# Layer 1's loop: one pair of three multiplies XW in 32 bits in tiles with one gathered tile, and the split of XW becomes a ring

## What is computed

```python
XW = X @ W
s_col = XW @ a[0, :f];  s_row = XW @ a[0, f:]
Z1 = leaky_relu(s_row[:, None] + s_col[None, :], 0.01)
den = exp(Z1)
num = A @ den
att = where(num != 0, den / num, 0)
H = A @ (att @ XW)
x = layernorm(x + H)
```

## Time and profile before

| | |
|---|---|
| median of 3 runs | 705.02 us (704.59 to 706.17) |
| profiled execution | 705.56 us, span 703.8 us |
| PE | 591.9 us busy, 84% of the span |
| DVE | 573.3 us, 81% |
| ACT | 442.3 us, 63% |
| POOL | 407.3 us, 58% |
| layer 1's loop | about 414 to 624 us of the span |

### The profile page before, as it was taken

One profiled execution on the slowest core, in us unless ns is written; L12 is line 12 of the kernel. 1 busy time (PEld: TensorE's weight loads), 2 busy tenths in 40 slices (PEclk: granted clock), 3 DMA queues, 4 the chain that ended last, 5 costly groups with the idle time before them and its releaser, 6 DMA issues.

```text
span 703.8 us, 11521 instructions
## 1 busy us (share of the span) xinstructions
PE 591.9 (84%) x4211; PEld 351.9 (50%) x4211; DVE 573.3 (81%) x1044; ACT 442.3 (63%) x689; POOL 407.3 (58%) x449
## 2 busy tenths in 40 slices
PE   4499999999999697999745988798989988868993
PEld 4343333333333296888635644344434444436883
DVE  1689999999999875578878866899999999985442
ACT  2378888888888551478995416777776777721000
POOL 5448888877778704445602163877576777002663
PEclk9999999999999769999955999999999999987998
DMA  9974444484000000000000041233232323000100
GB/s 146 101 78 41 40 36 37 37 297 150 1 1 1 5 2 8 16 24 17 17 9 12 13 116 50 74 105 87 68 91 77 97 72 84 17 5 8 30 28 16
DMA packets 17796, 37.20 MB, mean 53 GB/s; under 512 B 2570, under 2 KB 8222, under 8 KB 17726
## 3 DMA queue, kind: packets, MB, share of 16 engines
q0 software_dynamic: 7392, 24.32, 20.0%
q1 hardware_dynamic: 10334, 11.98, 5.2%
HBM read 48.72 MB, written 10.45 MB: 84 GB/s over the span
## 4 chain that ended last, share of the span: by engine, by line
PE 37%; DVE 35%; issue 15%; ACT 8%; POOL 2%; DMA 2%; DVEq 0%; POOLq 0%; ACTq 0%; SPq 0%
DVE ring L849 8%; PE PSALL L1727 8%; DVE R L858 7%; PE PSALL L1625 7%; PE PSALL L1440 6%; DVE ring L1255 4%; PE PSALL L1686 3%; ACT AW L603 3%; DVE ring L1248 3%; PE PSALL L1421 2%; PE PSALL L1371 2%; PE PSALL L1633 2%; ACT R L700 2%; DVE FR L1255 1%; PE PSALL L1499 1%
## 5 line engine op out<-in xcount | busy, mean ns | idle before, releaser
L399 POOL TENSOR_TENSOR R<-R,ring 128x452 f32<-128x452 f32 (+1 forms) x126 | 151.6, 1205 | 33.2 <-ACT ring L531 31.6
L858 DVE SCALAR_TENSOR_TENSOR R<-ring,R 128x452 bf16<-128x452 f32 (+1 forms) x132 | 134.6, 1021 | 0.0
L1421 PE MATMUL PSALL<-R,AO 128*128 128x452 bf16 (+2 forms) x396 | 99.5, 360 | 16.1 <-DVE R L858 15.1
L531 ACT ACTIVATE ring<-ring,sm 128x452 f32<-128x452 f32 (+1 forms) x132 | 88.4, 670 | 27.8 <-DVE ring L849 21.0
L1371 PE MATMUL PSALL<-XN 128*128 128x452 f16 (+2 forms) x396 | 99.3, 362 | 4.7 <-issue 4.2
L459 POOL DMA_INDIRECT AW<-ATd,FR x44 | 62.7, 1426 | 64.3 <-PE PSALL L1633 39.9
L1625 PE MATMUL PSALL<-AW,R 128*128 128x452 fp8e4 (+1 forms) x348 | 78.5, 357 | 24.9 <-DVE R L1187 18.6
L539 ACT ACTIVATE R<-ring,sm 128x452 bf16<-128x452 f32 (+1 forms) x132 | 88.6, 671 | 4.3
L849 DVE TENSOR_TENSOR ring<-PSALL,AT 128x452 f32<-128x452 f32 (+1 forms) x132 | 81.0, 613 | 0.9 <-PE PSALL L1371 0.9
L1686 PE MATMUL PSALL<-ring,X 128*128 128x452 bf16 (+1 forms) x300 | 67.8, 360 | 0.9 <-DVE ring L1255 0.9
L1421 PEld LDWEIGHTS PSALL<-R,AO 128*128 128x128 bf16 (+1 forms) x396 | 28.5, 97 | 76.2 <-DVE R L858 61.9
(11 more groups left out here) (253 smaller groups left out, 1033.1 us busy)
## 6 DMA issues: line engine op xcount, KB each, us to landing
AT<-in_adjT POOLq DMA_DIRECT2D x22, 338.5 KB, 7.7
ATd<-AT SPq DMA_DIRECT2D x2, 3723.5 KB, 17.3
XWd<-ring SPq DMA_DIRECT2D x11, 128.0 KB, 1.8
out<-ring SPq DMA_DIRECT2D x21, 64.0 KB, 1.5
AW<-ATd,FR POOLq DMA_INDIRECT x44, 4.3
X<-XWd,idx POOLq DMA_INDIRECT x22, 3.2
Wt<-in_W SPq DMA_DIRECT2D x1, 64.0 KB, 11.1
X<-in_x SPq DMA_DIRECT2D x1, 0.5 KB, 7.9
```

The lines of the kernel that those rows point to most:

```text
L399: i = G.tensor_tensor(ES_, ES_, z, ALU.add)
L858: V.scalar_tensor_tensor(F[0:rows, RW:RW + w], z, 1.0, F[0:rows, 0:w], ALU.subtract, ALU.subtract).then_inc(s_low, 1)
L1421: m = TE.matmul(PSALL[:, c, 0:w], half_[0:rows, jt, :], F[0:rows, o:o + w], start=(jt == 0 and k == 0), stop=(jt == T - 1 and k == 2))
```

## The change

- PE: the middle pair of a tile (`p % 3 == 1`) is multiplied by XW in 32 bits where `kinds[jt] == 0`: one matmul per chunk (`xw_full`) in place of three. The other pairs and the two-tile tiles keep the three (`xw_halves`). Two branches on PE choose.
- DVE: for that pair of a one-tile tile no low half is computed; a branch skips it, and a memset of one element reports it as done. The second gathered block's scores and halves are computed only if the next tile has two blocks, under a branch; the halves are one operation of 128 columns each. For that DVE loads `win[jt]` into a register, once a tile.
- ACT: the Exp of the denominators covers two blocks, and the third under a branch, with its own register load. The wait for DVE's scores stands before the branch.
- GpSimd: XW itself stays as it is in 32 bits; its halves go to a ring of four tiles, `XW2`, with two operations in place of three. From tile 4 on they wait until the products of tile t - 4 are through (`s_y`).

```diff
+        XW2 = sb("XW2", [P, 4, 2, D], BF16)
+        mark = sm[0:1, 13:14]
             def split_xw(t):
-                gp.wait_ge(s_ohl[0], T)
-                gp.wait_ge(s_perm[0], 1)
                 gp.wait_ge(s_AT[t], 32)
-                if t:
-                    gp.wait_ge(s_xws, 3 * t)
-                G.tensor_copy(iota[:, :], XWs[:, t, :]).then_inc(s_xws, 1)
-                gp.wait_ge(s_xws, 3 * t + 1)
-                G.tensor_tensor(XWh[:, t, :, 0], XWs[:, t, :], iota[:, :], ALU.subtract).then_inc(s_xws, 1)
-                gp.wait_ge(s_xws, 3 * t + 2)
-                G.tensor_copy(XWh[:, t, :, 1], iota[:, :]).then_inc(s_xws, 1)
+                if t >= 4:
+                    gp.wait_ge(s_y, 3 * (t - 3))
+                G.tensor_copy(XW2[:, t % 4, 1, :], XWs[:, t, :]).then_inc(s_xws, 1)
+                gp.wait_ge(s_xws, 2 * t + 1)
+                G.tensor_tensor(XW2[:, t % 4, 0, :], XWs[:, t, :], XW2[:, t % 4, 1, :], ALU.subtract).then_inc(s_xws, 1)
             def den_exp_small(jt):
+                kind = eng.value_load(win[0:1, jt:jt + 1], min_val=0, max_val=2)
                 av.wait_ge(s_denz, 3 * (jt + 1))
                 s = T + jt % 2 * DS
-                S.activation(den_w[:, s:s + DS, :], den_w[:, s:s + DS, :], ACT.Exp).then_inc(s_dene, 1)
+                met = av.covered()
+                with eng.If(kind == 1):
+                    S.activation(den_w[:, s + 2, :], den_w[:, s + 2, :], ACT.Exp)
+                av.only(met)
+                S.activation(den_w[:, s:s + 2, :], den_w[:, s:s + 2, :], ACT.Exp).then_inc(s_dene, 1)
+            def score(jt, q):
+                s = T + jt % 2 * DS
+                return V.tensor_scalar(den_w[:, s + 1 + q, :], cb3[:, jt, :], Rw[:, q, jt:jt + 1], r01w[:, q, jt:jt + 1],
+                                       ALU.add, ALU.max)
+            def half_of(jt, q):
+                s = T + jt % 2 * DS
+                return V.tensor_tensor(den_h[:, s + 1 + q, :, 0], den_w[:, s + 1 + q, :], den_h[:, s + 1 + q, :, 1], ALU.subtract)
-            def small_scores(jt):
+            def small_scores(jt, usual):
                 s = T + jt % 2 * DS
                 if jt >= 2:
                     dv.wait_ge(s_num, 6 * (jt - 1))
                 dv.wait_ge(s_pick, 2 if jt < FIRST else 4)
+                if usual:
+                    kinds[jt] = eng.value_load(win[0:1, jt:jt + 1], min_val=0, max_val=2)
+                    met = dv.covered()
+                    with eng.If(kinds[jt] == 1):
+                        score(jt, 1)
+                    dv.only(met)
+                    score(jt, 0).then_inc(s_denz, 2)
...
-            def small_halves(jt):
+            def small_halves(jt, usual):
                 s = T + jt % 2 * DS
                 dv.wait_ge(s_dene, jt + 1)
+                if usual:
+                    met = dv.covered()
+                    with eng.If(kinds[jt] == 1):
+                        half_of(jt, 1)
+                    dv.only(met)
+                    half_of(jt, 0).then_inc(s_denb, 1)
...
-            def attention_low(v):
+            def attention_low(v, general):
                 high, lower = halves_of(v)
                 dv.wait_ge(s_att1, v + 1)
-                V.tensor_tensor(lower, z_of(v), high, ALU.subtract).then_inc(s_alo, 1)
+                if general or v % 3 != 1:
+                    V.tensor_tensor(lower, z_of(v), high, ALU.subtract).then_inc(s_alo, 1)
+                else:
+                    met = dv.covered()
+                    with eng.If(kinds[v // 3] == 1):
+                        V.tensor_tensor(lower, z_of(v), high, ALU.subtract)
+                    dv.only(met)
+                    V.memset(mark, 0.0).then_inc(s_alo, 1)
+            def xw_full(p):
+                jt = p // 3
+                for q in range(2):
+                    c = 2 * (p % 3) + q
+                    m = TE.matmul(PSALL[:, c, 0:CH[c][1]], XWs[:, jt, :], z_of(p)[:, q * RW:q * RW + CH[c][1]],
+                                  start=(jt == 0), stop=(jt == T - 1))
+                m.then_inc(s_y, 1)
+            def xw_product(p, general):
+                jt = p // 3
+                pe.wait_ge(s_alo, p + 1)
+                pe.wait_ge(s_xws, 2 * (jt + 1))
+                if general or p % 3 != 1:
+                    xw_halves(p)
+                else:
+                    met = pe.covered()
+                    with eng.If(kinds[jt] == 0):
+                        xw_full(p)
+                    pe.only(met)
+                    with eng.If(kinds[jt] == 1):
+                        xw_halves(p)
+                    pe.only(met)
```

More of the change, by code:

```diff
@@ L1175, in small_scores @@
                 dv.wait_ge(s_pick, 2 if jt < FIRST else 4)
+                if usual:
[6 more added lines that the diff above has]
+                else:
+                    for q in range(WN):
+                        score(jt, q).then_inc(s_denz, 1)
                 V.tensor_scalar(den_w[:, s, :], cb3[:, jt, :], e_bias[:, jt:jt + 1], e_cap, ALU.add, ALU.min).then_inc(s_denz, 1)
-                for q in range(WN):
-                    V.tensor_scalar(den_w[:, s + 1 + q, :], cb3[:, jt, :], Rw[:, q, jt:jt + 1], r01w[:, q, jt:jt + 1],
-                                    ALU.add, ALU.max).then_inc(s_denz, 1)
-            def small_halves(jt):
+            def small_halves(jt, usual):
                 s = T + jt % 2 * DS
                 dv.wait_ge(s_dene, jt + 1)
-                V.tensor_tensor(den_h[:, s + 1:s + DS, :, 0], den_w[:, s + 1:s + DS, :], den_h[:, s + 1:s + DS, :, 1],
-                                ALU.subtract).then_inc(s_denb, 1)
+                if usual:
[5 more added lines that the diff above has]
+                else:
+                    V.tensor_tensor(den_h[:, s + 1:s + DS, :, 0], den_w[:, s + 1:s + DS, :], den_h[:, s + 1:s + DS, :, 1],
+                                    ALU.subtract).then_inc(s_denb, 1)
                 V.tensor_tensor(den_h[LOROWS:P, s, :, 1], den_w[LOROWS:P, s, :], den_h[LOROWS:P, s, :, 1],
@@ L1198, in den_scores @@
                 with eng.If(where["wide"] == 0):
-                    small_scores(jt)
+                    small_scores(jt, False)
                 dv.only(met)
@@ L1205, in den_halves @@
                 with eng.If(where["wide"] == 0):
-                    small_halves(jt)
+                    small_halves(jt, False)
                 dv.only(met)
@@ L1262, in layer1 @@
                     if v:
-                        attention_low(v - 1)
+                        attention_low(v - 1, general)
                     if jt + 1 < T:
@@ L1273, in layer1 @@
                             if cp == 0:
-                                small_scores(jt + 1)
+                                small_scores(jt + 1, True)
                             if cp == 1:
-                                small_halves(jt + 1)
+                                small_halves(jt + 1, True)
                     if v == 0:
@@ L1282, in layer1 @@
                         table(5)
-                attention_low(NV - 1)
+                attention_low(NV - 1, general)
             table(2)
@@ L1645, in wide_sums, with tile_sums @@
                     m.then_inc(s_num, 1)
+            def tile_sums(v):
+                small_sums(v, (0,))
+                met = pe.covered()
+                with eng.If(kinds[v // 3] == 1):
+                    small_sums(v, (1,))
+                pe.only(met)
+                table_sums(v)
             def num(v, general):
@@ L1660, in num, with xw_halves @@
                     pe.only(met)
[L1661 to L1667, removed]
+                    with eng.Else():
+                        tile_sums(v)
                     pe.only(met)
                 else:
[L1670 to L1677, removed]
+                    tile_sums(v)
+            def xw_full(p):
[5 more added lines that the diff above has]
+                m.then_inc(s_y, 1)
+            def xw_halves(p):
                 jt, high, lower = p // 3, *halves_of(p)
-                pe.wait_ge(s_alo, p + 1)
-                pe.wait_ge(s_xws, 3 * (jt + 1))
                 for q in range(2):
@@ L1685, in xw_product @@
                     for k, (part, att) in enumerate(((1, high), (1, lower), (0, high))):
-                        m = TE.matmul(PSALL[:, c, 0:CH[c][1]], XWh[:, jt, :, part], att[:, part_of],
+                        m = TE.matmul(PSALL[:, c, 0:CH[c][1]], XW2[:, jt % 4, part, :], att[:, part_of],
                                       start=(jt == 0 and k == 0), stop=(jt == T - 1 and k == 2))
                 m.then_inc(s_y, 1)
+            def xw_product(p, general):
[4 more added lines that the diff above has]
+                    xw_halves(p)
+                else:
+                    met = pe.covered()
+                    with eng.If(kinds[jt] == 0):
[3 more added lines that the diff above has]
+                        xw_halves(p)
+                    pe.only(met)
             def layer1(general):
```

6 lines of the change are left out of this document (4 added, 2 removed).

## The result

The changed kernel takes 701.65 us (median of 7 runs, 698.79 to 702.45) against 705.64 (704.59 to 707.85) for the kernel before in the same rounds: a ratio of 0.993, interval 0.9907 to 0.9953. Forecast were 700.3 us and -0.7%. The profiled execution took 698.98 us, with a span of 697.1.

The account below looks back on a forecast made before the run. One-tile tiles were taken as bound by a latency loop of 8.56 us, two-tile tiles by PE. Terms -4.6, -0.8, +0.2, +0.15 and +0.4 gave -4.7 us, from the median 705.02 to 700.3; range 696.5 to 708.0.

Parts of the forecast that it names:

- The loop that sets the period: One-tile tile: 2.37 us of PE and ACT latency, 6.16 of DVE in order and 0.03 make the 8.56 us period.
- the middle difference: DVE's low half of a one-tile tile's middle pair, 1.23 us: in the latency's shadow, so removing it saves nothing.
- Second score: DVE, one score operation fewer when the next tile has one gathered tile: 0.26 us off the loop.
- Halves: DVE, 128 columns instead of 256: gain 0.13 us; two operations for a two-tile successor: loss 0.20.
- tiles 2, 6 and 10: One-tile tiles followed by a two-tile tile: 0.20 - 0.12 = +0.08 us each, +0.2 together.
- GpSimd: Its split costs DVE's loop 0.24 us; with two operations, later in the tile, half is kept, 0.12.
- 32-bit pair: PE, two 32-bit matmuls take 1.52 us for 1.16, +0.36 a tile, hidden in PE's 1.35 idle.
- Tile 21: Nothing of a next tile is computed there, so the 32-bit pair's extra PE time shows: +0.4 us once.
- tiles 3, 7 and 11: Two-tile tiles: 0 followed by a one-tile tile (PE-bound), +0.05 us each followed by a two-tile tile.
- Control: Register loads, branches and waits on DVE and ACT: not shown in the loop, 0 us; 0.85 kept for a rival.
- Row fetches: GpSimd's fetches start about 3 us later but are needed nearly two tiles (17 us) after: hidden.
- rival D: Row fetches come late, a tile waits 1 to 3 us on line 1625 for a DMA: 702 to 712, chance 0.04.

Follow-up runs that it names:

- e3: Kernel before with the ring and the 32-bit pair, but both second scores and halves always computed: 705.28 us, 0.9974 of the kernel before.
- e1: Kernel before with only the ring (split in two GpSimd operations), gathered scores first, XW halves side by side: 704.06 us, 0.9957 of the kernel before.
- e6: e2 with the branches around the second scores and halves entered in one-tile tiles too: 704.96 us, 0.9976 of the kernel before.
- e8: e7 with the 32-bit pair only in one-tile tiles followed by a one-tile tile, never in tile 21: 696.14 us, 0.9846 of the kernel before.
- e4: The changed kernel itself, unedited, run and profiled once more: 701.93 us, 0.993 of the kernel before.
- e11: e8 with independent block sums issued ahead of tile 0's first sums, where PE idles: 697.61 us, 0.9871 of the kernel before.
- e2: Changed kernel without the 32-bit pair, every pair in three products and the middle difference computed: 698.98 us, 0.9889 of the kernel before.
- e7: Changed kernel with the next tile's scores issued ahead of the first pair's attention scores: 697.60 us, 0.9867 of the kernel before.

## Why the prediction was right, step by step

- **The loop that sets the period** (2.37 us of latency, then DVE in order). Right: the idle gap came where it was put (1.24 us, forecast about 1), DVE lost 26 us (forecast 25), and e3 against e1 shows the middle difference worth nothing. PE's idle at the tile start is 0.40 (forecast 0.5).
- **Second score**: forecast 0.26, measured 570.85 - 570.60 = 0.25, the one left.
- **Halves**: one of 128 columns taken as 0.33; it took 0.32 (565.38 to 565.70 in tile 15). Two were taken as 0.66 and take 0.54 on the mean (e6), +0.07 over one of 256 columns and not +0.20. This is one half of what went wrong for tiles 2, 6 and 10: forecast +0.08 each, measured 8.62 to 8.38 in tile 6, -0.24. The other half is the next point, since tile 6 falls to 8.37 with the ring alone (e1).
- **GpSimd**: half of 0.24 was kept as lost. All of it came back in tiles 16 to 18: e1 has 8.34, 8.32 and 8.32 there, and 8.32 in tile 20, where no split runs (tiles 4, 5, 9, 14 and 15 of e1 still take 8.38 to 8.43; what holds them is open). That is why the period of tile 16 is 7.94 and not 8.05. In tile 19, beside which no split ran before, the forecast was 0.39 and the measurement 8.32 - 7.90 = 0.42. The Trainium skill's "SBUF — State Buffer", "SBUF: two separate sides" tells of a lock held for a whole instruction; the prediction drew from it that two operations of three keep 0.16 of the 0.24, and that reading is not borne out, since 0.02 at most are left in tiles 16 to 19. The lock itself is not refuted: GpSimd's difference takes 0.43 us alone (415.10 in the changed kernel) and 1.25 at 566.22, until after the end of DVE's line 1277 at 567.13. Behind that line DVE has only the memset there, so that nothing on the loop is held up. It matters beside which DVE operation GpSimd's fall.
- **32-bit pair**: 1.52 forecast and measured, hidden in one-tile tiles. What I missed is where it runs: products lag three steps, so that the middle pair of tile t is multiplied in tile t + 1. Behind tiles 2, 6 and 10 that is a two-tile tile, in which PE has no idle time. This is the one step of the mechanism that the prediction had wrong: "it is hidden" holds for one-tile tiles only. Forecast for tiles 3, 7 and 11: 0, +0.05, +0.05; measured 9.65 against 9.39, 9.35 and 9.36. PE in tile 7 after, where the earlier trace rows had none but bf16 products:

```profile
489.60 1.69 PE L1662 MATMUL PSALL<-AW,R 128*128 128x452 fp8e4 x8
491.52 1.68 PE L1718 MATMUL PSALL<-ring,X 128*128 128x452 f32 x4
493.03 1.69 PE L1662 MATMUL PSALL<-AW,R 128*128 128x452 fp8e4 x8
```

  The pair from 489.60 takes 3.43 in place of 3.10. e8 takes this back (9.33).
- **Tile 21**: +0.4 forecast, 12.76 against 12.32 measured.
- **Control**: 0 forecast, and nothing measurable by e6, whose 0.05 a one-tile tile is the split of the halves. The Trainium skill's "Runtime: NRT & Kernel Launch", "Instruction fetch mechanics", would have allowed a few stalls; no row of the loop shows one.
- **Row fetches** (rival D): PE's first sums of a tile are released by DVE's halves or follow without a gap from tile 1 on, never by the DMA.

In sum the loop was forecast at -5.1 for tiles 1 to 20 (-4.7 with tile 21's +0.4) and came to -6.35: 0.9 more from the nine tiles beside a split (0.61 each on the mean, forecast 0.51), 1.0 more from tiles 2, 6 and 10, and 0.8 less from tiles 3, 7 and 11; the rest are some 0.05 a tile. **The forecast's median came out right partly by chance**: the loop with tile 21 gave 5.9, but the median fell by 4.0 only (5.45 in the rounds of e4). The table shows where such a difference lies: until tile 0, in tile 0 and behind the loop. The mean granted clock of each single execution sorts them. Of the changed kernel's seven, the two at 0.944 took 698.79 and 698.98 us, the five at 0.935 to 0.939 took 701.28 to 702.45. The kernel before, in the rounds of e1 to e11, took 704.66 to 705.53 at 0.944 or 0.945 and 707.38 to 707.84 at 0.937; the changed kernel with e4 took 701.47 to 702.51 at 0.935 to 0.937. Between like clocks the medians differ by 6.3 and by 5.5 us, on either side of the loop's 5.9. At 0.944 e2 took 697.82 and 698.25, some 0.9 less than the changed kernel, near the 0.75 of the loop. This is a comparison of what was recorded, not an experiment on the clock.

## What to carry to other kernels

In a software-pipelined loop, first find which operation closes it, and list what lies in the shadow of the latency: work taken out there gives nothing until other work on the path is moved into the hole (without the removal, e2, the loop was even 0.75 us shorter; once the scores were moved, the same removal was worth 2.2 to 2.7). Place each product in the tile in which it runs, not the one that it belongs to: a step that is hidden in its own tile can be bare in the next. And compare a loop by its own stretch of the trace, which repeats to 0.01 us here in two executions, before the whole span, of which tile 0 alone moved by 2.8 us without an edit.

## What was unexpected in the hardware

**The granted clock behind one and the same pause.** PE idles 3.0 us ahead of tile 0 in every kernel but those that fill it. The clock that it is granted afterwards differs. Stretches of 4 us (length, busy time of PE, PEld, DVE, ACT and POOL with counts, granted clock, DMA share, GB/s), before, after and e4 in that order:

```profile
416.00:420.00 4.00, 4.00 (x16) 2.17 (x15) 1.82 (x4) 1.71 (x3) 3.43 (x6) 0.75 0.21 41
```

```profile
416.00:420.00 4.00, 4.00 (x21) 2.22 (x20) 1.12 (x2) 1.60 (x3) 3.32 (x6) 1.00 0.27 90
```

```profile
416.00:420.00 4.00, 4.00 (x11) 1.73 (x10) 0.00 (x0) 0.89 (x2) 3.31 (x6) 0.50 0.36 103
```

and the first sums of tile 0, after and e4, which are the same program:

```profile
415.76 1.69 PE L1662 MATMUL PSALL<-AW,R 128*128 128x452 fp8e4 x8 [3.00 <-DVE R L1131]
```

```profile
415.53 3.17 PE L1662 MATMUL PSALL<-AW,R 128*128 128x452 fp8e4 x8 [3.01 <-DMA AW<-ATd,FR]
```

The same eight matmuls take 1.69 us at 2.4 GHz and 3.17 at 1.2, and tile 0 takes 18.81 or 21.64. Before had 20.50, with a clock of 0.75 in that stretch. So 2.8 us of span hang on how the clock stands when the gather lands. Ahead of it, in code that the change doesn't touch, PE multiplies 44 blocks by the identity, back to back; before, after and e4 in that order:

```profile
381.08 6.47 PE L1563 MATMUL PSALL<-ident,st 128*128 128x128 f32 x44
```

```profile
382.22 7.17 PE L1600 MATMUL PSALL<-ident,st 128*128 128x128 f32 x44
```

```profile
381.12 8.04 PE L1600 MATMUL PSALL<-ident,st 128*128 128x128 f32 x44
```

The granted clock in 384 to 388 was 1.00, 0.69 and 0.60. In e4 these 44 account for 1.57 of the 1.64 us by which tile 0 starts later than before, in the changed kernel's first profile for 0.70 of 1.87; the other 1.14 had come up ahead of 381 us. That the clock makes up the spread between the medians is borne out by the mean clocks of the single executions above, but only one execution of each kernel (two of the changed one) was profiled: which stretch it was in the others is not shown. Why the clock stood otherwise there in the changed kernel's executions is open.

**A register load and branches cost DVE 0.66 us bare and nothing measurable covered**: 0.66 to 0.71 in tiles 16 to 20 of e7 and 0.74 to 0.76 in tiles 16 to 18 of e8 (whose branch needs the kinds of two tiles), ahead of the first score, against no gap ahead of the scores in e6, where a difference of 1.2 us is queued ahead.
